# Queries, keys and row maxima turned on VectorE in 32x32 blocks instead of on TensorE, with the tokens of a half batch in another order

## The reference

```python
x = x + 0.5 * _L0_ffn_ref(_layernorm(x))
x = x + _L0_attn_ref(_layernorm(x))
x = x + 0.5 * _L0_ffn_ref(_layernorm(x))
...
q, k, v = (x @ w.T).reshape(B, T, 16, 16)
q, k = rope(rms(q)), rope(rms(k))
attn = softmax(einsum('bhtd,bhsd->bhts', q, k) * scale + 1.0)
y = einsum('bhts,bhsd->bhtd', attn, v) @ wproj.T
```

## Time and profile before

| | us |
|---|---|
| median of 3 runs (2161.29 to 2164.03) | 2162.02 |
| the profiled execution, its own time | 2166.2 |
| its span in the trace | 2164.4 |
| the attention loop, 64 steps | 192 |
| busy in the 192 us from 913 to 1105: TensorE, VectorE, ScalarE | 191.84, 165.77, 167.10 |

### The profile page before, as it was taken

The page is one execution under the profiler, slowest core; times in us unless marked ns, Lnnn a source line. Parts: engine busy times, 40 slices in busy tenths (PEclk is TensorE's granted clock), DMA queues, the critical chain, the costliest instruction groups (busy, mean ns, idle before and its releaser), DMA issues.

```text
span 2164.4 us, 39604 instructions
## 1 busy us (share of the span) xinstructions
PE 2085.6 (96%) x14643; PEld 1079.0 (50%) x14643; DVE 1731.9 (80%) x2562; ACT 1679.3 (78%) x3251; POOL 990.4 (46%) x1221
## 2 busy tenths in 40 slices
PE   5799999999999999999999999999999999997997
PEld 4588974433444444444444444444444333246987
DVE  7776768988879888988988898889889889535774
ACT  5566646898888888988898898889888888745664
POOL 5787538552751672285168227614840101104542
PEclk9799998999999999999999999999999999999999
DMA  7454413346334434335433434434442435203331
GB/s 249 141 188 168 147 59 76 77 101 113 76 80 84 89 96 100 68 86 121 78 78 80 100 66 92 100 85 84 78 108 46 88 42 119 59 6 128 118 126 60
DMA packets 137857, 208.94 MB, mean 97 GB/s; under 512 B 30527, under 2 KB 95295, under 8 KB 137408
## 3 DMA queue, kind: packets, MB, share of 16 engines
q1 hardware_dynamic: 129792, 189.14, 36.8%
q0 software_dynamic: 7680, 16.87, 2.5%
q10 hardware_dynamic: 192, 0.39, 0.1%
HBM read 128.87 MB, written 72.01 MB: 93 GB/s over the span
## 4 chain that ended last, share of the span: by engine, by line
PE 75%; DVE 7%; ACT 1%; issue 1%; DMA 1%; SPq 0%; POOL 0%; POOLq 0%; ACTq 0%; DVEq 0%
PE PS L1146 23%; PE PS L1129 18%; PE PS L1112 14%; PE PS L1019 6%; DVE NMX L2401 4%; PE PS L826 3%; PE PS L1083 3%; PE PS L983 1%; PE PS L981 1%; PE PS L982 1%; PE PS L961 1%; PE PS L963 1%; PE PS L962 1%; PE PS L1154 1%; DMA KF<-qs 0%
## 5 line engine op out<-in xcount | busy, mean ns | idle before, releaser
L2401 DVE TENSOR_REDUCE NMX<-PS 128x1 f32<-128x1024 f32 x1024 | 1225.4, 1218 | 199.0 <-PE PS L1112 183.0
L1559 ACT ACTIVATE PB<-PS 128x512 f32<-128x512 f32 x2048 | 1104.4, 604 | 149.7 <-PE PS L1129 112.7
L1129 PE MATMUL PS<-QF,KF 51*128 51x512 f32 x2048 | 775.4, 458 | 4.1 <-ACT PB L1559 1.0
L1112 PE MATMUL PS<-KF,QF 49*128 49x512 f32 x2048 | 734.0, 447 | 8.2 <-DVE NMX L2401 6.4
L1146 PE MATMUL PS<-PB,V 128*17 128x512 f32 (+1 forms) x5776 | 583.8, 476 | 0.2
L1129 PEld LDWEIGHTS PS<-QF,KF 51*128 51x128 f32 x2048 | 317.2, 185 | 417.7 <-ACT PB L1559 226.4
L1112 PEld LDWEIGHTS PS<-KF,QF 49*128 49x128 f32 x2048 | 312.2, 186 | 163.9 <-DVE NMX L2401 91.3
L1146 PEld LDWEIGHTS PS<-PB,V 128*17 128x17 f32 x5776 | 96.4, 95 | 236.1 <-issue 162.9
L2040 DVE TENSOR_TENSOR HLR<-HL,HHR 128x512 fp32r<-128x512 f32 x128 | 92.5, 724 | 85.7 <-ACT HHR L1475 80.2
L981 PE MATMUL PS<-W2H,HLR 128*128 128x256 f32 x512 | 143.0, 279 | 0.0
L983 PE MATMUL PS<-W2H,HHR 128*128 128x256 f32 x512 | 141.7, 277 | 0.0
(11 more groups left out here) (351 smaller groups left out, 3101.6 us busy)
## 6 DMA issues: line engine op xcount, KB each, us to landing
W<-in_w SPq DMA_DIRECT2D x32, 1024.0 KB
QF<-qs SPq DMA_DIRECT2D x186, 128.0 KB
KF<-qs SPq DMA_DIRECT2D x186, 128.0 KB
qs<-HI SPq DMA_DIRECT2D x64, 256.0 KB, 2.1
qs<-R1R SPq DMA_DIRECT2D x62, 256.0 KB, 2.3
QX<-x2d SPq DMA_DIRECT2D x8, 1024.0 KB, 5.4
out_x<-QX SPq DMA_DIRECT2D x8, 1024.0 KB, 4.8
YT<-YU SPq DMA_DIRECT2D x124, 64.0 KB, 3.6
```

Of the source, the lines that this page charges most:

```text
L1112: m = e.matmul(PS[:, 2 * i + half, :], QF[k][at:at + ROWS_S, p * SEQ + ti * 128:p * SEQ + ti * 128 + 128], KF[k][at:at + ROWS_S, p * SEQ + ...
L1129: e.matmul(PS[:, bank, :], KF[k][at:at + ROWS_ST, p * SEQ + sbk * 128:p * SEQ + sbk * 128 + 128], QF[k][at:at + ROWS_ST, p * SEQ + th * 51 ...
L1559: e.activation(PB[j % 3][:, h * 512:(h + 1) * 512], PS[:, place["e", tile], :], ACT.Exp).then_inc(e_out, 1)
L2401: e.tensor_reduce(NMX[:, u % 2, at:at + 1], PS[:, 2 * i:2 * i + 2, :], AX.XY, ALU.max, negate=True).then_inc(s_max, 1)
```

## The change

For batches 1 to 7 a piece of `split` is one VectorE transpose of 128x512 in 32x32 blocks, from QR into R1 in SBUF; ScalarE then makes one copy (HI from R1) instead of two from PSUM, and TensorE and the PSUM bank have no part in it. Such a transpose leaves each block of 32 tokens in its own group of 32 partitions, so a piece has four groups of 32 rows which hold, in turn, every fourth run of 32 tokens. The stores to qs become four DMAs for each of the two parts, with runs of 128 tokens (512 bytes), and the tokens of a half batch stand in another order in Q and K. So that the values match, V17 is written to a new DRAM tensor `vs` and read back by eight DMAs in the new order; the router columns in the old order are read from there too, into XR (before this they were taken from V17). The result YU is put back in order by the copy that takes it out of PSUM (`spread_back`). Batch 0 keeps its old way of splitting. For all 32 units the maxima are turned on VectorE as well (three small instructions at steps 16, 16.5 and 17), and `load_max` becomes eight DMAs of 128-byte runs.

```diff
+        def stored_in(m):
+            return 32 * min(m, 4) + 128 * max(m - 4, 0)
...
+        def spread_back(u, dst, src):
+            if u < 4:
+                return dst, src
+            return (dst.rearrange("p (t i r) -> p i t r", t=4, i=4), src.rearrange("p (i t r) -> p i t r", i=4, t=4))
...
+                        dims = qs_d[b % 2][pc, j * 128:(j + 1) * 128, hf * 512:(hf + 1) * 512]
+                        if b == 0:
+                            e.dma_start(dims, src.bitcast(F32)).then_inc(st_q[k % 2], 16)
+                        for i in range(4 if b else 0):
+                            e.dma_start(dims[:, i * 128:(i + 1) * 128].rearrange("(g d) n -> d g n", d=32),
+                                        src[32 * i:32 * i + 32, :].bitcast(F32).rearrange("d (g n) -> d g n", n=128)
+                                        ).then_inc(st_q[k % 2], 16)
...
             def load_max(u):
-                e.wait_ge(mt_out, u + 1)
                 for pc in range(2):
-                    for ab in range(2):
-                        row = 64 * ab + ROWS_S + pc
-                        e.dma_start(QF[u % 3][row:row + 1, :].bitcast(F32).rearrange("q (a n) -> q a n", n=128),
-                                    MT[16 * ab:16 * ab + 16, u % 2, pc, :].bitcast(F32)).then_inc(ld_m[u % 3], 16)
+                    e.wait_ge(mt_out, 3 * u + 2 + pc)
+                    rows_q = QF[u % 3][ROWS_S + pc:128:64, :].bitcast(F32).rearrange("s (a i q) -> s a i q", i=4, q=32)
+                    for i in range(4):
+                        e.dma_start(rows_q[:, :, i, :], MT[32 * i:32 * i + 32, u % 2, pc, :].bitcast(F32)
+                                    ).then_inc(ld_m[u % 3], 16)
...
+            def key_rows(b):
+                yield values_at(b, 7) + 3
+                e.wait_ge(v_out, 8 * (b + 1))
...
+                e.dma_start(v_d.rearrange("(t p) f -> p t f", p=128), V17[b % 2][:, :, :, :].rearrange("p t h f -> p t (h f)")[:, :, 0:ROW_V]
+                            ).then_inc(st_v, 16)
+                yield values_at(b, 7) + 6
+                e.wait_ge(st_v, 16 * b)
+                for hf in range(2):
+                    for q in range(4):
+                        at = hf * 512 + q * 128
+                        e.dma_start(V17[b % 2][32 * q:32 * q + 32, 4 * hf:4 * hf + 4, :, :].rearrange("r i h f -> r i (h f)")[:, :, 0:ROW_V],
+                                    v_d[at:at + 128, :].rearrange("(i r) f -> r i f", r=32)).then_inc(ld_v, 16)
+                if b < NB - 1:
+                    yield BATCH * b - BEGIN[b] + 6
+                    e.wait_ge(xl_out, b)
+                    e.dma_start(XR[:, :, :], v_d.rearrange("(t p) f -> p t f", p=128)[:, :, 17 * H:17 * H + NE]
+                                ).then_inc(ld_v, 16)
...
-            def maxima(u):
-                yield 16
-                e.wait_ge(s_max, 32 * u + 32)
-                bank = ring("mt", u)
-                take(bank)
-                e.transpose(PS[0:32, bank, 0:128], NMX[:, u % 2, :], IDN).then_inc(mt_full, 1)
...
-                    e.copy(hi_of(n), PS[:, place["split", n], :])
-                    e.copy(raw_of(n), PS[:, place["split", n], :]).then_inc(sp_raw, 1)
+                    if b == 0:
+                        e.copy(hi_of(n), PS[:, place["split", n], :])
+                        e.copy(raw_of(n), PS[:, place["split", n], :]).then_inc(sp_raw, 1)
+                    else:
+                        e.copy(hi_of(n), raw_of(n)).then_inc(sp_raw, 1)
...
             def maxima(u):
-                yield UNIT + 1
-                e.wait_ge(mt_hi, u + 1)
+                yield 16
+                e.wait_ge(s_max, 32 * u + 32)
+                e.transpose(MR[:, p, :], NMX[:, p, :]).then_inc(mt_out, 1)
+                yield 16.5
+                e.wait_ge(mt_out, 3 * u + 1)
...
+                e.tensor_copy(MT[:, p, 0, :], MR[:, p, :]).then_inc(mt_out, 1)
+                yield 17
+                e.wait_ge(mt_out, 3 * u + 2)
                 e.tensor_tensor(MT[:, p, 1, :], MR[:, p, :], MT[:, p, 0, :].bitcast(F32), ALU.subtract
                                 ).then_inc(mt_out, 1)
...
+            def split(b):
+                for k, at, hf, j, m in pieces(b):
+                    n = 8 * b + k
+                    yield at
+                    e.wait_ge(rope_out[hf], 4 * b + 8)
+                    e.wait_ge(st_q[n % 2], stored_in(n // 2))
+                    e.transpose(raw_of(n).rearrange("d (g t r) -> d g t r", g=4, t=4),
+                                QR[:, 4 * hf:4 * hf + 4, j * 128:(j + 1) * 128].rearrange("p t (g d) -> p g t d", g=4)
+                                ).then_inc(sp_full, 1)
```

More of the change, by code:

```diff
@@ L29 @@
 ROW, SENT = 524, 260
+ROW_V = 17 * H + NE
 WIDE = D + NE
@@ L273, in build_program @@
         NMX = sb("NMX", [128, 2, 32])
-        MT = sb("MT", [32, 2, 2, 128], F32R)
-        MR = sb("MR", [32, 2, 128])
+        MT = sb("MT", [128, 2, 2, 32], F32R)
+        MR = sb("MR", [128, 2, 32])
         RS = sb("RS", [128, 3, 8])
@@ L282, in build_program @@
         XL = sb("XL", [128, 8, NE])
+        XR = sb("XR", [128, 8, NE])
         RQ = sb("RQ", [128, 2, 128])
@@ L785, in sync_program @@
                     side.begin(BEGIN[1], before(1))
+                    side.begin(BEGIN[1], key_rows(1))
                 for k in range(2, NB):
@@ L788, in sync_program @@
                         side.begin(n + 3, before(k))
+                        side.begin(n + 3, key_rows(k))
                 if r == 0 and 1 <= b <= NB:
@@ L805, in sync_program @@
                     for i in range(2):
-                        e.wait_ge(st_q[i], 128 * NB)
+                        e.wait_ge(st_q[i], stored_in(4 * NB))
                     load_w(NE)
@@ L1086, in post @@
                     busy[bank] = (pj_out, 8 * b + t + 1)
-            def maxima(u):
-                yield 16
-                e.wait_ge(s_max, 32 * u + 32)
-                bank = ring("mt", u)
-                take(bank)
-                e.transpose(PS[0:32, bank, 0:128], NMX[:, u % 2, :], IDN).then_inc(mt_full, 1)
-                busy[bank] = (mt_hi, u + 1)
             def score(n, i, half):
@@ L1333, in tensor_program @@
                     side.begin(n, split(0))
-                    prepare(side, BEGIN[1], 1, pre_x, split, values)
+                    prepare(side, BEGIN[1], 1, pre_x, None, values)
                 for k in range(2, NB):
                     if n == BEGIN[k]:
-                        prepare(side, n, k, pre_x, split, values)
+                        prepare(side, n, k, pre_x, None, values)
                 if r == 0 and 1 <= b < NB:
@@ L1342, in tensor_program @@
                     side.begin(n, leaving())
-                if n % UNIT == 0 and n < NS:
-                    side.begin(n, maxima(n // UNIT))
                 j = n - LAG
@@ L1533, in copied_v @@
                         e.wait_ge(pv_full, 64 * (b - 1))
-                        e.wait_ge(xl_out, b - 1)
+                        if b == 2:
+                            e.wait_ge(xl_out, 1)
                 e.copy(V17[b % 2][:, t, :, 0:16],
@@ L1544, in post @@
                     e.copy(QX[:, t, 0:WIDE], PS[:, place["pj", 8 * b + t], 0:WIDE]).then_inc(pj_out, 1)
-            def maxima(u):
-                yield 16
-                e.wait_ge(mt_full, u + 1)
-                if u >= 2:
-                    e.wait_ge(ld_m[(u - 2) % 3], 64 * ((u - 2) // 3 + 1))
-                e.copy(MT[:, u % 2, 0, :], PS[0:32, place["mt", u], 0:128])
-                e.copy(MR[:, u % 2, :], PS[0:32, place["mt", u], 0:128]).then_inc(mt_hi, 1)
             def exponential(j, i):
@@ L1572, in weighed @@
                         e.wait_ge(rope_free, th + 1)
-                    e.copy(YU[:, th, :], PS[:, V_BANK, :]).then_inc(pv_out, 1)
+                    e.copy(*spread_back(u, YU[:, th, :], PS[:, V_BANK, :])).then_inc(pv_out, 1)
             def leaving():
@@ L2463, in vector_program @@
                 if n == 0:
-                    prepare(side, BEGIN[1], 1, pre_x)
+                    prepare(side, BEGIN[1], 1, pre_x, split)
                 for k in range(2, NB):
                     if n == BEGIN[k]:
-                        prepare(side, n, k, pre_x)
+                        prepare(side, n, k, pre_x, split)
                 if r == 0 and 1 <= b < NB:
```

32 lines of the change are left out of this document (20 added, 12 removed).

## The result

The changed kernel takes 2197.09 us (median of 4 runs, 2192.31 to 2203.69) against 2161.67 us: a ratio of 1.0155, 95% interval 1.0135 to 1.0175. The profiled execution spans 2195.6 us against 2164.4, 31.2 us more, and 30.6 of these lie between the first maximum of the attention loop and its last.

What follows compares the result with a forecast made beforehand. In bare steps VectorE, ScalarE and TensorE were taken as even, with side work lengthening steps. Terms -17.5 - 5 + 2 + 25.5 + 7 = +12 us gave 2178 profiled, 2174 us median; range 2132 to 2201.

Steps and rivals of the forecast that it cites:

- both mechanisms that the prediction named: Batch ends: TensorE's first weight waits about 4 us for maxima rows; pieces: VectorE's transposes wait about 1 us a batch for stores.
- my own case: Whole kernel: small gain at pieces, outweighed by SP's queue at batch ends; 2174 us, range 2158 to 2192, chance 0.43.
- pieces, without waits for stores: 56 pieces of batches 1 to 7: transposes moved to VectorE save 2.5 us a batch, 17.5 us, between 0 and 52.
- maxima on VectorE, and their rows landing later: 32 turns of maxima: 5 us off, between 0 and 10; their rows landing later cost 2 us, between 0 and 22.
- values in front of the maxima rows: SP's queue at five batch ends: eight value DMAs delay the maxima rows; 5.1 us each, 25.5 us on, between 2 and 40.
- stores in four parts: Pieces' stores, eight DMAs for two: VectorE's transposes wait for them; 1 us a batch, 7 us, between 0 and 21.
- the clock's price at the batch ends: Behind TensorE's halt at each of five batch ends: lower granted clock, 0.9 us added to 4.2 us of wait.
- Rival (b): Whole kernel faster: batch end costs 0.4 us, pieces give 4 us a batch, TensorE and PSUM ring limit; 2131 us, chance 0.34.
- The transposes: VectorE at the pieces: a 128x512 transpose takes 0.70 us, back to back as little as 0.65.
- rival (c): Much slower: VectorE bounds through 1.2 us transposes, or store waits of 3 us a batch, and issues at 0.87; 2200, chance 0.16.
- That VectorE has little more room than TensorE: Attention loop pieces: 0.23 us gained each where VectorE lacks slack, 0.4 us at steps 17, 19, 33 and 34.
- at nothing: Reordered copy of YU, load of XR and store of the values: each taken to cost no time.

Runs made afterwards that it cites:

- both: Changed kernel with V's reads issued behind the maxima rows and each piece's two parts stored by one whole DMA each; 2126.01 us, 0.9848.
- maxima alone: Kernel before the change, with only the maxima turned on VectorE and their eight DMAs of 128-byte runs put in; 2149.24 us, 0.9959.
- the covered kernel: Changed kernel, with TensorE given 14 matmuls of ones into a spare bank before the five weights that wait for late maxima rows; 2189.07 us, 1.0117.
- the kernel with the values later: Changed kernel, with the eight reads of the values issued by SP after the maxima rows of the batch's last unit instead of before; 2160.12 us, 1.0004.
- second transpose: VectorE makes each piece's 128x512 transpose twice, against the kernel with V's reads late and pieces evenly spaced; 2206.31 us, 1.0202.
- the kept turns: TensorE still makes four 128x128 transposes of constants per piece, against the kernel with V's reads late and pieces evenly spaced; 2185.02 us, 1.0106.
- the even one: Changed kernel with V's reads late and pieces three steps apart but for the first two, closer in batch 1; 2183.54 us, 1.0083.

## Why the prediction was off

The sign was right, both mechanisms that the prediction named were there, and the wide range held the time; but 2197 lies above my own case's range of 2158 to 2192. Term by term, against what the runs measured:

| term | predicted | measured |
|---|---|---|
| pieces, without waits for stores | -17.5 | -24 (both - maxima alone) |
| maxima on VectorE, and their rows landing later | -5 + 2 | -8.9 (maxima alone) |
| values in front of the maxima rows | +25.5 | +29.4 to +32.6 |
| stores in four parts | +7, at most 21 | +33.7 to +37.0 |

- **The step that failed** is the price of the stores in four parts: "I take 1 us for a batch, 7 us in all, between 0 (all landed in time) and 3 us a batch, 21 us." The runs have 33.7 to 37.0 us for it. It is mis-sized fivefold, and its upper bound by more than half. The wait itself was not so far off: 19.9 us in 8 places are 2.8 a batch, next to the upper bound of 3. What was wrong with the wait is that I let the fourth piece's stores begin as early as before, and said that "The next two pairs follow as closely", where the third piece's eight DMAs and SB now come right before them: the fourth piece's exact part was issued 7.6 us after its transpose. The greater part is that I took the clock's price at the batch ends but not here, though the halt is of the same kind: 34 to 37 us for 20 to 21 us of waiting, 1.6 to 1.9 us for each, and next to nothing above the wait in the loops where the clock stayed at 1.00.
- **The batch end** came out near its number by another make-up. Predicted were 4.2 us of wait and 0.9 of clock; measured were 16.5 / 5 = 3.3 us of wait and, by the covered kernel, 1.0 to 2.5 of clock. In the trace the steps 3 and 4 are 4.6 to 6.3 us longer at these five ends, 28.0 in all, which fits. The other 4.6 of the 32.6 us lie away from the ends: the kernel with the values later is also 2.4 us shorter in the loop of batch 0 and 3.5 behind the attention loop, and gives some back elsewhere. The issue prices (0.5 and 0.605 taken, 0.47 and 0.55 measured) and the 8.8 us for sixteen DMAs (8.2) held. Rival (b) had this at 0.4 us and falls.
- **The transposes**: 0.70 us taken, 0.702 measured. The large-reduction price of rival (c), 1.2 us, and with it the estimate from the Trainium skill, page "VectorE: DVE Perf Modes", section "The three transpose paths", 1.24 us for four small ones, fall: 128x512 as one instruction is not four of 128x128. Rival (c)'s total, 2200, was nonetheless nearest to the result, by its other half: "waits for stores at 3 us a batch".
- **That VectorE has little more room than TensorE** held in the sum and not by place, so part of its good number is luck. The kernel with both edits less the maxima alone gives the gain of each piece, the same within 0.05 us in the loops of batches 2 to 6: 0.1 us for the pieces at 17 and 19 together, where I had 0.8; 1.0 for those at 25 and 28, where I had 0.46; 1.0 for 30 and 31, where I had 0.46; 1.1 for 33 and 34, where I had 0.8. At 17 and 19, where I saw VectorE idle beside projections, its second transpose cost 0.7 us in full, so it has no room there. Together that is 3.3 us a batch in place of 2.5, and the term was undersized by 6.5 us. On TensorE's side the kept turns cost 1.8 us a batch at three places, and their sum stays open.
- **The maxima** gained 6 us more than forecast, 3.9 of them from a stretch of low clock in the last batch that the kernel before happens to have the earlier trace rows; I had that row and used it only as a price.
- Of what goes "at nothing", only the sum was tried: the kernel with both takes the copy of YU, XR and the store of the values along, and still gains 33 us.

Moving V's reads behind the maxima rows and setting the pieces further apart makes the change what it could be: 0.9907 and 0.9902, 20 us faster than before. With whole stores it would be 0.9848, but for tokens out of order.

## What to carry to other kernels

Before cutting a DMA in four, add up the issues of its queue between the transfer's data and the next instruction that waits for it, everything else in that queue included, at every place of the table: a queue that issues at 0.45 to 0.55 us apiece is an engine too, and here it fell behind at one place in each batch while the stores' bytes stayed the same. Look as well for what the queue waits for, in order, just before that place: four idle microseconds stood there. A place where TensorE halts for 2 to 3 us cost between once and nearly three times its wait here: ask of each new wait what clock follows it, and prefer the table without halts to the even one. When two costs and a gain are mixed, run the four combinations of the two costs first; here they showed that the two add up, and how large the gain is without them.

## What was not expected of the hardware

- A halt of two to three microseconds was enough in most places, not in all, to lower the granted clock to about half for the next stretch (0.52 to 0.54 over seven microseconds). Waits of 2.1 to 2.8 us cost 2.3 us where the clock stayed at 1.00 and up to 7.1 where it was 0.63 over the 14 us behind. With TensorE kept at useless work through the halt the clock stayed up at four of five places.
- The stores in four parts, with 512-byte runs in place of 2 KB ones, raised the packets from 164050 to 212435 (the kernel before has 137857), and this in itself cost little: with the pieces further apart and all packets in place, the loops of batches 2 to 6 are each 0.5 to 0.6 us longer than with whole stores.
- Time also came and went at places that no edit touched. The part behind the attention loop takes 293.2 us in one of these runs and 305.6 in another, at a granted clock of 0.97 and 0.94, and the low stretch of the last batch is worth 4 us. Differences of that size between two versions are not the edit's own until the traces have been compared stretch by stretch.
